# A fused decoder layer on one core: loads issued one batch further ahead, more staging buffers, transposes moved, and a new order table

## The reference

```
x = x + rg_lru(layernorm(x))                      # u, g = x Wi, sigmoid(x Wg); scan over the tokens; Wo
x = x + cross_attention(ctx, layernorm(x))        # 8 heads of 128; keys: 722 rows of ctx and the 100 latents
x = x + ffn(layernorm(x))                         # 8 experts, each token goes to one; gelu(x W1) W2

# cross attention of one batch
xn, ln = layernorm(ctx) * g + b, layernorm(x) * g2 + b2
q      = (ln Wq + bq) * 128 ** -0.5
k, v   = concat(xn, ln) Wkv + bkv
out    = softmax(q k^T) v Wo + bo
```

## Time and profile before

| | us |
|---|---|
| three runs | 1274.63 median (1272.57 to 1274.74) |
| the profiled execution | 1274.87 |
| its span in the trace | 1273.1 |
| PE busy | 1117.5 (88%) |
| DVE busy | 762.5 (60%) |
| ACT busy | 512.4 (40%) |

### The profile page before, as it was taken

The page is one execution under the profiler, slowest core; times in us unless marked ns, Lnnn a source line. Parts: engine busy times, 40 slices in busy tenths (PEclk is TensorE's granted clock), DMA queues, the critical chain, the costliest instruction groups (busy, mean ns, idle before and its releaser), DMA issues.

```text
span 1273.1 us, 19270 instructions
## 1 busy us (share of the span) xinstructions
PE 1117.5 (88%) x6660; PEld 1001.7 (79%) x6661; DVE 762.5 (60%) x1448; ACT 512.4 (40%) x945; POOL 161.4 (13%) x138
## 2 busy tenths in 40 slices
PE   2878779799799799799799799799998499999996
PEld 2857677799699699699699699699896387878875
DVE  6789515574473574574484483484543786683992
ACT  3322335343233233233233243233333385674871
POOL 6415520000000000000000000000000121131222
PEclk9988998899899899999999999999999599999998
DMA  9010636600300300300300300300202698593980
GB/s 311 16 66 27 217 127 221 237 1 1 121 0 0 121 0 0 121 0 0 120 1 0 120 1 0 117 3 0 80 1 80 203 342 281 177 342 108 345 299 27
DMA packets 72289, 134.71 MB, mean 106 GB/s; under 512 B 12205, under 2 KB 20909, under 8 KB 71232
## 3 DMA queue, kind: packets, MB, share of 16 engines
q1 hardware_dynamic: 70496, 129.49, 29.7%
q0 software_dynamic: 1760, 4.79, 1.1%
HBM read 114.57 MB, written 20.67 MB: 106 GB/s over the span
## 4 chain that ended last, share of the span: by engine, by line
PE 65%; DVE 14%; DMA 12%; issue 4%; ACT 2%; SPq 1%; POOL 0%; DVEq 0%; POOLq 0%; ACTq 0%
PE bank L518 15%; PE bank L519 15%; PE bank L520 14%; DMA raw<-in_ctx 6%; PE bank L958 6%; PE bank L965 4%; DMA stage<-in_W 3%; PE bank L933 3%; PE bank L899 2%; DVE wsl L1284 1%; ACT wsh L1206 1%; DVE pt_l L1284 1%; DVE str__62 L1259 1%; DMA scr_tokens<-x2b 1%; PE bank L950 1%
## 5 line engine op out<-in xcount | busy, mean ns | idle before, releaser
L518 PE MATMUL bank<-pt_h,xn_h 128*128 128x256 f32 (+1 forms) x576 | 176.2, 306 | 48.4 <-DVE pt_l L1284 48.3
L520 PE MATMUL bank<-pt_h,xn_l 128*128 128x256 f32 (+1 forms) x576 | 170.4, 296 | 0.0
L519 PE MATMUL bank<-pt_l,xn_h 128*128 128x256 f32 (+1 forms) x576 | 170.4, 296 | 0.0
L1284 DVE TENSOR_TENSOR wsl<-stage,wsh 128x2048 fp32r<-128x2048 f32 x64 | 145.5, 2289 | 22.2 <-ACT wsh L1206 20.1
L518 PEld LDWEIGHTS bank<-pt_h,xn_h 128*128 128x128 f32 x576 | 114.5, 199 | 52.5 <-issue 44.1
L1137 ACT ACTIVATE pr<-bank,smx 128x412 f32<-128x412 f32 x48 | 29.0, 604 | 284.5 <-DVE smx L1437 284.5
L518 PE MATMUL bank<-xt_h,qt_h 128*128 128x410 f32 (+1 forms) x384 | 137.3, 358 | 1.2 <-ACT c L1194 1.0
L1206 ACT CAST wsh<-stage 128x2048 fp32r<-128x2048 f32 x64 | 122.5, 1916 | 36.8 <-DMA stage<-in_W 25.5
L519 PE MATMUL bank<-xt_l,qt_h 128*128 128x410 f32 (+1 forms) x384 | 134.9, 351 | 0.0
L520 PE MATMUL bank<-xt_h,qt_l 128*128 128x410 f32 (+1 forms) x384 | 134.6, 351 | 0.0
L519 PEld LDWEIGHTS bank<-pt_l,xn_h 128*128 128x128 f32 x576 | 115.0, 200 | 0.0
(11 more groups left out here) (228 smaller groups left out, 2520.1 us busy)
## 6 DMA issues: line engine op xcount, KB each, us to landing
stage<-in_W SPq DMA_DIRECT2D x64, 1024.0 KB, 7.2
scr_q<-st SPq DMA_DIRECT2D x16, 800.0 KB, 3.6
qf<-scr_q SPq DMA_DIRECT2D x8, 1600.0 KB, 8.8
raw<-in_ctx SPq DMA_DIRECT2D x8, 768.0 KB, 10.6
raw<-in_ctx SPq DMA_DIRECT2D x8, 512.0 KB
wq<-in_Wq SPq DMA_DIRECT2D x1, 2048.0 KB, 17.0
wk<-in_WkT SPq DMA_DIRECT2D x1, 2048.0 KB, 9.1
wv<-in_Wv SPq DMA_DIRECT2D x1, 2048.0 KB, 8.0
```

What stands on the lines that cost most here:

```text
L518: pe.matmul(dest, lh, rh, start=start and k == 0, stop=False)
L519: pe.matmul(dest, lh, rl, start=False, stop=False)
L520: last = pe.matmul(dest, ll, rh, start=False, stop=stop and k == n - 1)
L1284: return dve.tensor_tensor(dst, src, high.bitcast(F32), ALU.subtract)
```

## The change

There are five edits.

- SP's loop is written anew. The loads for batch 1 are issued ahead of it, and body b issues those for batch b+2: `load_first` (queries, bias rows, first part of the context) before it waits for Y of batch b, `load_second` (second part, latents) after that.
- There are five staging buffers: the first half uses four in turn, the second half three. The fifth lies over `xh`, and its first use waits until the latents have been written to DRAM.
- `latents(1)` stands behind the 32 units "k" of the first half on PE and ACT, and DVE's `low_rows` of batches 4 to 7 too. In the first two heads of the first half ACT copies all four units.
- SP writes the last four `xin` right behind the eight staging writes of the first half.
- The table `plan` has another order. "PT" 1 stands ahead of "B+" 0; "R" 0 and "B+" 1 come later; "L+" 0 stands behind the four Z of group 0; "V" 1 stands between "PT" 4 and "PT" 5; "Q+" 1 and "Q+" 3 come later.

```diff
--- before.py
+++ after.py
@@ -261,6 +261,15 @@
     st = [mem.over(hs_h, f"st{k}", [P, HALF, ND, T], skip=k * HALF * ND * T) for k in range(2)]
+    st += [mem.over(w3[2], f"st{k}", [P, HALF, ND, T], skip=(k - 2) * HALF * ND * T) for k in (2, 3)]
+    st.append(mem.over(xh, "st4", [P, HALF, ND, T], skip=B * D - HALF * ND * T))
+    ring = [[0, 1, 2, 3], [0, 1, 4]]
+
+    def stage_of(half, h):
+        k = ring[half][h % len(ring[half])]
+        earlier = [(i, j) for i in range(2) for j in range(HEADS) if (i, j) < (half, h) and
+                   ring[i][j % len(ring[i])] == k]
+        return k, len(earlier)
     wq = mem("wq", [P, ND, INNER])
@@ -350,7 +359,7 @@
     s_tpl, s_tel, s_qp, s_qe, s_out_a = sem("s_tpl"), sem("s_tel"), sem("s_qp"), sem("s_qe"), sem("s_out_a")
-    s_qout = [sem("s_qout0"), sem("s_qout1")]
+    s_qout = [sem(f"s_qout{k}") for k in range(5)]
     s_apart = sem("s_apart")
@@ -387,12 +396,12 @@
-    plan = [("B+", 0), ("PT", 1), ("S", 2), ("R", 0), ("S", 3), ("N", 2), ("Z", (0, 0)), ("B+", 1), ("N", 3), ("S",
...
+    plan = [("PT", 1), ("B+", 0), ("S", 2), ("S", 3), ("N", 2), ("R", 0), ("B+", 1), ("Z", (0, 0)), ("Z", (0, 1)),
...
@@ -443,7 +452,6 @@
     norms += [("A", 2), ("A", 3), ("B", 2), ("B", 3), ("C", 2), ("C", 3)]
-    norms += [("H", b) for b in range(HALF, B)]
     obank = [bank[6], bank[7], bank[0], bank[1], bank[2], bank[3], bank[6], bank[7]]
@@ -454,7 +462,7 @@
         early[1, 2 * k + 1] = early.get((1, 2 * k + 1), []) + [("Q", k)]
-    by_act = [what == "q" or dc % 2 == 0 for what, _, _, dc in q_units]
+    by_act = [what == "q" or dc % 2 == 0 or (half, h) < (0, 2) for what, half, h, dc in q_units]
@@ -595,22 +603,24 @@
                     acts, dves = stage_rows(half, h)
+                    k, _ = stage_of(half, h)
                     sp.wait_ge(s_qe, acts)
                     sp.wait_ge(s_qd, dves)
                     sp.dma_start(d_q[half * HALF:(half + 1) * HALF, :, h * ND * T:(h + 1) * ND * T].rearrange(
-                        "b p n -> p b n"), st[h % 2][:].rearrange("p b c t -> p b (c t)")).then_inc(s_qout[h % 2], 16)
+                        "b p n -> p b n"), st[k][:].rearrange("p b c t -> p b (c t)")).then_inc(s_qout[k], 16)
+                if not half:
+                    write_residuals(range(HALF, B))
                 sp.wait_ge(s_ce, half + 1)
                 sp.dma_start(d_c[half * HALF:(half + 1) * HALF, :].rearrange("b (h t) -> h b t", h=HEADS),
                              c8[0:HEADS, half, :].rearrange("h (b t) -> h b t", b=HALF)).then_inc(s_cout, 16)
                 if not half:
                     sp.wait_ge(s_op, B)
-                    for s in s_qout:
-                        sp.wait_ge(s, 16 * HEADS // 2)
+                    for k in range(4):
+                        sp.wait_ge(s_qout[k], 16 * HEADS // 4)
                     load_queries(0)
                     sp.wait_ge(s_cout, 16)
                     sp.wait_ge(s_padq, 1)
                     load_bias_rows(0)
-                    write_residuals(range(HALF, B))
@@ -622,27 +632,25 @@
-            def batch(b, events):
-                more = ("T+", 0) in events
-                if more:
-                    sp.wait_ge(s_qread, (b + 1) * 3 * ND)
-                    load_queries(b + 1)
-                    sp.wait_ge(s_xnl, b * KC + MC // 2)
-                    load_context(b + 1, 0)
-                    sp.wait_ge(s_xnl, b * KC + KC)
-                    load_context(b + 1, 1)
-                    load_latents(b + 1)
-                    sp.wait_ge(s_cqfree, b + 1)
-                    load_bias_rows(b + 1)
-                else:
-                    sp.wait_ge(s_qread, B * 3 * ND)
-                    load_weights(0, 0, range(2))
-                    sp.wait_ge(s_vused, 1)
-                    load_weights(0, 0, range(2, 4))
+            def load_first(b):
+                sp.wait_ge(s_qread, b * 3 * ND)
+                load_queries(b)
+                sp.wait_ge(s_cqfree, b)
+                load_bias_rows(b)
+                sp.wait_ge(s_xnl, (b - 1) * KC + MC // 2)
+                load_context(b, 0)
+
+            def load_second(b):
+                sp.wait_ge(s_xnl, b * KC)
+                load_context(b, 1)
+                load_latents(b)
+
+            def finish(b):
                 sp.wait_ge(s_x2, b + 1)
                 sp.dma_start(d_tok[bass.ds(b * T, T), :], x2b[0:T, :]).then_inc(s_x2out, 16)
-                if more:
-                    sp.dma_start(x1b[0:T, :], d_x1[b + 1]).then_inc(s_x1l, 16)
+
+            def next_rows(b):
+                sp.dma_start(x1b[0:T, :], d_x1[b]).then_inc(s_x1l, 16)
@@ -651,8 +659,20 @@
-            batches(sp, batch)
-
+            load_first(1)
+            load_second(1)
+            with sp.Fori(0, B - 2) as b:
+                load_first(b + 2)
+                finish(b)
+                next_rows(b + 1)
+                load_second(b + 2)
+            sp.wait_ge(s_qread, B * 3 * ND)
+            load_weights(0, 0, range(2))
+            finish(B - 2)
+            next_rows(B - 1)
+            sp.wait_ge(s_vused, 1)
+            load_weights(0, 0, range(2, 4))
+            finish(B - 1)
@@ -847,8 +867,6 @@
                     u += 1
-                if not half:
-                    latents(1)
                 for h in range(HEADS):
@@ -860,6 +878,7 @@
                 if not half:
+                    latents(1)
                     pe.wait_ge(s_x1, B)
@@ -1175,28 +1194,30 @@
                                    ).then_inc(s_qe, 1)
-                    if h == HEADS - 1 and not half:
-                        latents(1)
-                    elif h == HEADS - 1:
+                    if h == HEADS - 1 and half:
                         act.wait_ge(s_out_a, 16 * B)
                         act.wait_ge(s_lnout, 16 * B)
                 elif by_act[u]:
-                    n = half * HEADS + h
-                    if n >= 2:
-                        act.wait_ge(s_qout[h % 2], 16 * (n // 2))
+                    k, uses = stage_of(half, h)
+                    if uses:
+                        act.wait_ge(s_qout[k], 16 * uses)
+                    elif k == 4:
+                        act.wait_ge(s_lnout, 16 * B)
                     act.wait_ge(s_qp, u + 1)
-                    act.activation(st[h % 2][:, :, dc, :], bank[u % 4][:, 0:HT].rearrange("p (b t) -> p b t", b=HALF),
+                    act.activation(st[k][:, :, dc, :], bank[u % 4][:, 0:HT].rearrange("p (b t) -> p b t", b=HALF),
                                    ACT.Identity, scale=float(DH) ** -0.5).then_inc(s_qe, 1)
                 if what == "k" and dc == ND - 1:
                     run(0, early.get((half, h), []))
                 if (what, h, dc) == ("k", HEADS - 1, ND - 1):
+                    if not half:
+                        latents(1)
                     act.wait_ge(s_cp, half + 1)
                     act.activation(c8[0:HEADS, half, :], zbank[half][0:HEADS, 0:HT], ACT.Identity,
                                    scale=float(DH) ** -0.5).then_inc(s_ce, 1)
             act.activation(warm[:, 1:2], warm[:, 0:1], ACT.Exp)
             act.wait_ge(s_cout, 16 * 2)
-            for s in s_qout:
-                act.wait_ge(s, 16 * HEADS)
+            for k in range(5):
+                act.wait_ge(s_qout[k], 16 * sum(stage_of(i, j)[0] == k for i in range(2) for j in range(HEADS)))
@@ -1530,15 +1551,20 @@
                 elif what == "k":
-                    n = half * HEADS + h
+                    k, uses = stage_of(half, h)
                     if not by_act[u]:
-                        if n >= 2:
-                            dve.wait_ge(s_qout[h % 2], 16 * (n // 2))
+                        if uses:
+                            dve.wait_ge(s_qout[k], 16 * uses)
+                        elif k == 4:
+                            dve.wait_ge(s_lnout, 16 * B)
                         dve.wait_ge(s_qp, u + 1)
-                        dve.tensor_scalar(st[h % 2][:, :, dc, :], bank[u % 4][:, 0:HT].rearrange("p (b t) -> p b t", b=HALF),
+                        dve.tensor_scalar(st[k][:, :, dc, :], bank[u % 4][:, 0:HT].rearrange("p (b t) -> p b t", b=HALF),
                                           float(DH) ** -0.5, None, ALU.mult).then_inc(s_qd, 1)
                     if dc == ND - 1:
                         run(0, early.get((half, h), []))
+                        if (half, h) == (0, HEADS - 1):
+                            for b in range(HALF, B):
+                                low_rows(b, B + b, tbank[b % 2], s_tel)
             dve.wait_ge(s_cp, 2)
```

## The result

| | before | after |
|---|---|---|
| median of the compared runs, us | 1274.68 (1272.57 to 1276.54) | 1215.67 (1210.01 to 1217.41) |
| profiled execution, us | 1274.87 | 1210.01 |
| its span, us | 1273.1 | 1208.2 |
| PE busy | 88% | 91% |

The ratio is 0.953 (95% interval 0.949 to 0.957), 59 us less. The forecast was 1213 us with a range of 1203 to 1227.

The account below looks back on a forecast made before the run. PE, busy 88% of the span, was taken as the bound, held up by six waits for `pt_l`. From 1274.87 us, 53.9 + 9.1 + 1.5 - 3 = 61.5 gives 1213.4, stated as 1213; range 1203 to 1227, the forecast's own 1205 to 1222.

Parts of the forecast that it names:

- The six waits: Loop bodies: PE's six waits for `pt_l` go, 41.5 us plus 12.4 of low clock, 53.9 together; body 97.59 to about 88.
- The step on the second part of the context: Loop bodies: issued behind Y, it lands at 334 to 341; it may land at 344 and cost nothing.
- The joint: Where the groups meet, PT 4 to the last group's first Z: idle 1.6 to 2.2 us, clock loss 3 (gain 4 to loss 6).
- that rule: At the joint: frequent short idle times between matmul groups make the clock go back and forth; by it the loss is 6 us.
- Query stage, first half: Units "k": PE stands still from 141.6 to about 146.7 for a staging write; 1.5 us gained, ends -1 and +8.
- Second half: Query stage: ACT's 8.17 us wait goes, 2.2 of clock saved, a 1.2 us wait for DVE comes; 9.1 us gained.
- First body: Bias rows go ahead of the context, which lands 0 to 3.8 us later; covered by PE's products, cost 0, up to 3.8 uncovered.
- the bias rows would hold the context up: First body: 800 single elements at about 10.5 ns each, 8.4 us; about 1 to 2 us would reach PE, once.
- the rivals: Late work in bodies 1228 us (0.15); query stage gives nothing 1224 (0.08); half the waits stay 1240 (0.03); slower 1285 (0.02).

Follow-up runs that it names:

- the repeat: The changed kernel run again with no edit, timed against the kernel before: median 1216.70 us, ratio 0.9534; its profiled execution took 1218.32 us.
- the added products: Changed kernel plus matmuls whose result nobody reads, five behind PT 5 and three behind PT 6: 1204.75 us, ratio 0.944 to 0.946 against the kernel before.

## Why the prediction was right, and where its steps were off

**The six waits.** Forecast: all gone, 53.9 us with their clock, the body at 88. Measured: none left, bodies of 88.4 to 88.5. The six bodies gave 48.9 us, and their joints took 6 x 1.52 - 2.55 = 6.6 more than before, so the waits were worth 55.5; the repeat gives the same (50.5 + 5 x 1.52 - 2.55). The cause is shown by the two halves run apart: early loads with the old order 1214.9, the new order with late loads 1266.6. The text had ascribed part of it to the order ("with `pt_l` ahead of the context, PE goes from S 3 straight into Z"). That part was wrong: the order moves the wait to another product and shortens it from 6.9 to 5.9 us on average (41.46 and 35.3 over six). The step on the second part of the context held: DVE waits for no part of the context in the six bodies.

**The joint.** Idle time as forecast (1.83 us, forecast 1.6 to 2.2). Its clock was forecast at a loss of 3, at most 6. In the profile after it is 6 x 1.52 + 2.7 = 11.8 us, against 4.2 before (1.64, 1.26 and 1.29 in three bodies, the first among them): a loss of 7.6. In the repeat it is 6 x 1.52 + 1.5 = 10.6, a loss of 6.4. Both lie beyond the step's own end of 6. And its reason, both waits in one place, fell: with the waits apart again it is five bodies of seven. Each joint behind which the clock fell cost 1.52 us, too, and not the 1.3 of the step. Why it falls more often than before stays open. That the long waits are gone isn't enough of a reason: with the queue program of before they stand in each of the six bodies, and Z (2, 0) is slow in seven of seven. Nor is the order: with that of before it is five. The Trainium skill ("TensorE: Matmul & The Clock Gate", "A second HAM failure mode: psum-queue depth-cycling") has the clock go back and forth on short idle times between groups; the added products, which take these idle times away and hold the clock at 1.00, agree with it. The 6 us that the prediction gave by that rule were nearer than my 3.

**Query stage, first half.** Forecast: one wait of about 5 us near 142 and 1.5 gained. Measured: nothing gained (59.3 us before and after, 59.6 in the repeat). The wait is there, ending at 142.06, at 7.03 us. The profiled execution was 7.35 ahead by then, so in the clock of before it ends at 149.4 and not at 146.7. The first staging write came at 133.77 + 7.35 = 141.1, as the step had it. What failed is the landing: 7.65 us until ACT had the buffer back (133.77 to 141.42), where I took the 5.9 of before. The run with the staging writes first shows that nearly all of this wait comes from the order in SP's queue (0.4 us is left), and the run with the transposes in the old place that these 4 us were there to be had without moving them.

**Second half.** Forecast: 8.17 gone, 1.2 us in its place, 9.1 gained. A wait of 1.19 stands at 178.97, in before's clock 186.3 (forecast 186), and 9.2 are gained in both traces. The two halves together were forecast at 10.6; by the traces they gave 9.2 and 8.95, by the run without them 10.8.

**First body.** Forecast 0; measured 1.6 and 0.5. Behind its joint the clock fell before (1.64) and not in the profile after; in the repeat it fell again. The wait for `wo` went the other way, from 5.0 to 6.6 and 5.2 us. What makes up the rest I didn't trace. DVE's wait for the context of batch 1 costs PE nothing, as said, and still costs nothing at 6.61 us. From the figure of the Trainium skill ("DMA: Bandwidth & Descriptors", "Bandwidth"), about 10.5 ns for each packet of transfers issued from GpSimd, the prediction had estimated that the bias rows would hold the context up by 8.4 us. The trace doesn't show that: from the issue of the queries to the context's arrival the stretch is short and full of bytes, 299 GB/s at a DMA share of 0.88:
```profile
217.66:227.37 9.71, 6.85 (x33) 6.80 (x34) 1.46 (x3) 1.07 (x2) 0.00 (x0) 0.70 0.88 299
```
That is 2.9 MB, mostly the queries (1.6), the first part (0.77) and some of the second; 8.4 us of delay have no room in it. The next loads show it more plainly: the queries are issued at 286.06 and the two bias transfers at 286.63 and 287.21, and over all batches their median times to landing are 6.6, 5.9 and 5.9 us, so the bias rows land within some 0.5 us of the queries ahead of them.

**The sum.** Forecast 61.5. The repeat has 55.5 - 6.4 + 8.95 and nothing to speak of elsewhere, 57.9, less 1.2 at the start. The forecast of 1213 stands 2.7 us below the median. The joint was under-sized by 3 to 5 us and the query stage over-sized by 1.5, against 1.6 more from the waits. That the 1.6 us offset a part of the other two is luck. The forecast's own range is worked out wrongly at its low end: the ends of its terms (4 gained at the joint, 8 in the first half) give 1213 - 7 - 6.5 = 1199.5 and not 1205; the high end of 1222 comes out. None of the rivals came about; nothing late shows inside the bodies.

## What to carry to other kernels

When an engine waits for a transfer once per turn of a loop, issue that transfer a turn earlier before reordering the work around it: the loads alone did all here, the order nothing. When cover is counted in products of PE, follow each of them through the engines that must give its banks back; the cover ends at the first one whose engine stands in the same wait. And ask of each wait in a busy stretch what the clock does behind it: filling 1.8 us of idle time a body with matmuls that nobody needs bought 11 to 12 us over eight bodies.

## What the runs showed of the hardware

- The granted clock behind the same two short waits (1.16 and 0.67 us) was 1.00 in one body and 0.61 in the next of one execution, with 2.88 and 4.42 us for the same product. Two waits of 1.07 and 1.14 us, with the transposes of one row tile between them as well, were followed by 7.00 us at 0.50, where the same product takes 3.64 us in the changed kernel.
- With no idle time in the bodies the clock stayed at 1.00 for 521.67 us.
- The start of the program, before anything that was changed, varies by 8.6 us between two profiled executions of one kernel (97.73 and 106.32). Eight identical normalizations on DVE (L1333) took 8.93 us in one and 10.87 in the other, the load of `x` was 1.8 us later, and the clock was lower. PE's busy time in a part of this stretch, with the clock as third number behind the length, first of the short start and then of the long one:
```profile
33.91:45.00 11.09, 11.09 (x61) 1.00 0.07 12
```
```profile
39.73:51.00 11.27, 11.27 (x47) 0.73 0.01 1
```
  Why is open. A gain of a few microseconds should be read stage by stage and not off one execution's end.
- A write of 13 KB (`c`) took 7.8 us to land with 3 MB of weights and three staging writes ahead of it in SP's queue, and 1.5 us in the changed kernel, without the weights. The last of the staging writes took 13.5 us, against a median of 5.2 in the changed kernel.
- 768 single elements (the larger of the two bias transfers) took a median of 5.9 us to land and came in with the 1.6 MB that had been issued 0.6 us ahead of them.
